# x split into its four phases by strided copies on 32 partitions, in place of a block transpose and a TensorE transpose

## The chip, the cores and the metric

The kernel runs on one core of a Trainium2 chip. The metric is the time of one execution on the device, in microseconds (us), as the median of several runs. TensorE, VectorE, ScalarE and GpSimd are called PE, DVE, ACT and POOL in the profile, and SP is the engine whose queue issues most of the loads.

## The reference

x has the shape (128, 32, 512): 128 samples, 32 channels, length 512. Two layers are added to it, each a conditioned mixing of channels and a feed-forward part.

```python
# layer 0
h = conv1d(x, weight, kernel 9, pad 4, 4 groups of 8 channels) + (cond @ c_weight.T)[:, :, None] + fside
logits = h @ W_gate + b_gate                 # over the length: D = 512, 8 experts
top 2 experts of each of the 4096 tokens (sample, channel)
x = x + mean over the 2 of relu(h @ W_e[e] + b_e[e])
# layer 1
att = softmax(mlp(cond))                     # 8 kernels
g = einsum(att-mixed 32x32 kernel, x) + att @ bias_k
x = x + g @ dequant(qweight, scales, zeros) + bias     # int4 weights, 512 x 512
```

## The kernel before, in words

The 128 samples are taken in NG = 32 groups of SUB = 4, so that a group is 128 tokens (sample, channel) of length 512. There are three stages.

**Stage 1, one step for each group.** The convolution is done on TensorE with time on the contraction's other side: the length is cut into PH = 4 phases (position l is 4 i + q), and `phases[q * 32 + channel, buffer, sample, 1 + i]` holds them, with a zero column at either end. Three shifts of that tile against the weights `wconv` give the convolution of one sample, so a group takes 4 x 3 matmuls into `ps_conv`. Around it, a group a goes through these steps:

- SP loads x of the group into `xt[:, a % 4, :]` (a ring of XR = 4), 128 rows of 2 KB (L376, L403).
- VectorE transposes it in blocks of 32 x 32 into `ring_a` (`transpose_x`, L694), reading every fourth element.
- TensorE transposes `ring_a` in four pieces into the PSUM bank `ps_ph` (`transpose_phases`, L1098).
- ScalarE copies `ps_ph` into `phases` (L567).
- TensorE convolves (L1169). VectorE adds the context: `hT` (L807).
- TensorE multiplies `hT` with the gate weights and an identity beside them (`gate_and_rows`, L1157). This gives the logits and the rows of h back in token order. The next group's gate waits for `tok_ready`, ScalarE's two copies of those rows into `token_list` (L584), and for VectorE's `partial` sums (L816).
- VectorE finds the top 2 experts, TensorE counts ranks (L1143, L1144), VectorE works out the two row numbers (L845), ScalarE copies the token's keys (L574), and GpSimd scatters the rows into the experts' lists in DRAM with two indirect DMAs (L524).

The order on each engine is written out by hand. In step g TensorE does: convolution g, transposes of g + 1, ranks of g - 2, gate of g - 1. VectorE does: hT g, block transpose g + 2, then the small operations of g - 1 and g - 2. ScalarE does: phases g + 1, keys g - 2, rows g - 1. `phases` and `ring_a` have two buffers each. In the last groups (from 24 on) a small network on the conditions runs between these steps, with two table loads and three activations on ScalarE (L600, L603, L606).

SP's queue loads x of group a + 4 once group a is transposed; between them it issues the experts' weights (1 MB a time, L385), the context (L400) and zeroed list heads (L390).

**Stage 2.** The lists are worked off in 71 blocks of 128 tokens: SP loads a block from the lists into a slot of `xt` (`list_step`, four loads L434 and one of keys L437), VectorE transposes it (L921), TensorE multiplies it with its expert's weights (L1196), VectorE adds the bias (L935), ScalarE applies the ReLU (L620), GpSimd scatters the results. On VectorE the first list transposes stand between the last steps of stage 1: list 0 comes ahead of step 30, list 1 ahead of step 31. The list loads of the first four blocks wait until the slots of `xt` have been read, through `xT_ready`.

**Stage 3** adds the two results of each token to x and does layer 1.

Program text that matters: before its first step TensorE, VectorE and ScalarE prepare the convolution's weights: ScalarE and VectorE pick the taps with six small copies each (`pick_taps`, L363), 32 partitions x 128 elements read 60 bytes apart.

## Time and profile before

| | us |
|---|---|
| median of 3 runs | 514.61 (514.56 to 514.78) |
| the profiled execution: its own time | 515.17 |
| the profiled execution: span of the trace | 513.4 |
| TensorE busy | 496.1 (97%) |
| VectorE busy | 347.0 (68%) |
| ScalarE busy | 121.0 (24%) |
| GpSimd busy | 153.3 (30%) |

Busy shares are means over three stages with different loads. Stage 1 reaches from the start to about 150 us, stage 2 to about 395 us. "PEld" is the loading of TensorE's stationary operand, which overlaps its matmuls. The granted clock is 1.00 at TensorE's full speed.

### The profile page before, as it was taken

What the parts mean: (1) busy time and instruction counts of PE and PEld (TensorE: products, weight loads), DVE (VectorE), ACT (ScalarE), POOL (GpSimd) and SP (SyncE); (2) the same over time, 40 slices, a digit from 0 to 9 for tenths busy, and PEclk for the clock granted to TensorE, in tenths of its full rate; (3) what the DMA queues carried; (4) which work ended last, traced back from release to release, by engine and by line L of the source; (5) the groups of instructions that cost most, each with busy time, mean ns of one, the idle gap of its engine ahead of it and who ended that gap; (6) DMA issues with size and microseconds to landing.
All of it is one profiled execution on the core that took longest, in us unless ns stands there. A gap on an engine that the chain in (4) does not pass through costs nothing. (4 is left out here: it accounts for less than half of the span.)

```text
span 513.4 us, 10342 instructions
## 1 busy us (share of the span) xinstructions
PE 496.1 (97%) x2412; PEld 329.5 (64%) x2413; DVE 347.0 (68%) x1082; ACT 121.0 (24%) x277; POOL 153.3 (30%) x178
## 2 busy tenths in 40 slices
PE   6999999999999999999999999999997999999996
PEld 5999999999964444444444444444544676767674
DVE  4588888888866547573354445444445899999996
ACT  3232333334421111111111111111123222222220
POOL 9144444444447322233323323332224000000000
PEclk9999999999998999999999999999999999999999
DMA  4969978999885686676665767675554798888852
GB/s 111 290 216 291 274 270 287 324 364 324 235 220 165 200 229 156 166 203 172 176 176 162 184 163 200 163 188 158 150 147 141 252 343 278 288 284 281 296 180 102
DMA packets 91442, 113.07 MB, mean 220 GB/s; under 512 B 25438, under 2 KB 62222, under 8 KB 90372
## 3 DMA queue, kind: packets, MB, share of 16 engines
q1 hardware_dynamic: 73200, 71.26, 49.3%
q0 software_dynamic: 11664, 36.24, 19.3%
q10 hardware_dynamic: 6536, 5.10, 3.5%
q8 instruction: 16, 0.26, 0.2%
q14 instruction: 26, 0.21, 0.1%
HBM read 67.55 MB, written 46.52 MB: 222 GB/s over the span
## 5 line engine op out<-in xcount | busy, mean ns | idle before, releaser
L1196 PE MATMUL bank<-we,lT 128*128 x536 | 233.6, 597 | 1.7 <-DVE ring_a L935 1.6
L1196 PEld LDWEIGHTS bank<-we,lT 128*128 128x128 f32 x536 | 101.7, 191 | 129.0 <-issue 128.8
L935 DVE TENSOR_TENSOR ring_a<-bank,be_bc 128x512 f32<-128x512 f32 x71 | 48.9, 690 | 104.4 <-PE bank L1196 50.4
L541 POOL DMA_INDIRECT pairs_d<-ring_b,pair_i x71 | 71.1, 1002 | 161.3 <-DVE pair_i L924 113.7
L1169 PE MATMUL bank<-wconv,phases 128*128 128x128 f32 x768 | 91.8, 276 | 0.7 <-ACT phases L567 0.7
L620 ACT ACTIVATE ring_b<-ring_a 128x512 f32<-128x512 f32 x71 | 44.7, 631 | 196.7 <-DVE ring_a L935 181.5
L1169 PEld LDWEIGHTS bank<-wconv,phases 128*128 128x128 f32 x768 | 89.1, 193 | 0.9 <-ACT phases L567 0.9
L524 POOL DMA_INDIRECT lists_d<-token_list,row_i x64 | 62.9, 983 | 83.6 <-DVE row_i L845 50.1
L921 DVE STREAM_TRANSPOSE lT<-xt 128x512 f32<-128x512 f32 x71 | 49.8, 702 | 5.7 <-DMA keys<-lists_d 5.4
L1263 PE MATMUL bank<-wq,high 128*128 128x512 f32 x128 | 37.4, 414 | 3.4 <-PEq L1211 3.4
L1157 PE MATMUL bank<-wg,lT 128*128 128x136 f32 x256 | 37.4, 289 | 1.1 <-DVE partial L816 1.1
L694 DVE STREAM_TRANSPOSE ring_a<-xt 128x512 f32<-128x512 f32 x32 | 35.3, 1102 | 0.0
L1267 PE MATMUL bank<-wq,low 128*128 128x512 f32 x128 | 34.5, 391 | 0.0
L567 ACT COPY phases<-bank 128x512 f32<-128x512 f32 x32 | 19.2, 600 | 64.5 <-PE bank L1098 49.2
L807 DVE TENSOR_TENSOR lT<-bank,rows_r 128x512 f32<-128x512 f32 x32 | 22.1, 690 | 16.3 <-PE bank L1169 13.1
L1157 PEld LDWEIGHTS bank<-wg,lT 128*128 128x128 f32 x256 | 31.8, 190 | 1.3 <-issue 1.2
L1242 PE MATMUL bank<-mix_bd,we 128*128 128x128 f32 x224 | 32.2, 287 | 0.0
L1242 PEld LDWEIGHTS bank<-mix_bd,we 128*128 128x128 f32 x224 | 27.3, 191 | 5.7 <-DVE we L1048 5.6
L584 ACT COPY token_list<-bank 128x256 f32<-128x256 f32 x64 | 20.7, 376 | 31.0 <-issue 17.1
L1267 PEld LDWEIGHTS bank<-wq,low 128*128 128x128 f32 x128 | 24.0, 188 | 5.5
L675 ACT CAST high<-bank 128x512 fp32r<-128x512 f32 x32 | 18.7, 586 | 36.3 <-PE bank L1242 36.3
L1263 PEld LDWEIGHTS bank<-wq,high 128*128 128x128 f32 x128 | 21.8, 190 | 7.0 <-issue 4.2
(194 smaller groups left out, 401.4 us busy)
## 6 DMA issues: line engine op xcount, KB each, us to landing
xt<-lists_d SPq DMA_DIRECT2D x284, 64.0 KB
xt<-in_x SPq DMA_DIRECT2D x60, 256.0 KB, 4.1
we<-pairs_d SPq DMA_DIRECT2D x28, 512.0 KB, 4.8
we<-in_L_ffn_W_e SPq DMA_DIRECT2D x8, 1024.0 KB
out<-orow_list SPq DMA_DIRECT2D x32, 256.0 KB, 2.8
lists_d<-orow_list SPq DMA_DIRECT2D x8, 257.0 KB
be_bc<-in_L_ffn_b_e ACTq DMA_DIRECT2D x4, 512.0 KB
words<-pairs_d POOLq DMA_DIRECT2D x4, 512.0 KB, 5.4
```

The lines of the kernel that those rows point to most:

```text
L524: pool.indirect_dma_start(lists_d, bass.IndirectOffsetOnAxis(ap=row_i[:, j, k:k + 1], axis=0), token_list[:, j, :], None, bounds_check=E * ...
L541: pool.indirect_dma_start(pairs_d, bass.IndirectOffsetOnAxis(ap=pair_i[:, s % DR:s % DR + 1], axis=0), ring_b[:, s % U, :], None, bounds_c ...
L620: act.activation(ring_b[:, j, :], ring_a[:, j % 2, :], ACT.Relu, scale=0.5).then_inc(result_ready, 1)
L694: dve.transpose(ring_a[:, ja % 2, :].rearrange("m (h q i) -> m q h i", h=MH, q=PH), xt[:, ja, :].rearrange("c (h l q) -> c q h l", h=MH, q ...
L921: dve.transpose(lT[:, ja, :].rearrange("m (p h r) -> m h p r", p=PH, h=MH), xt[:, ja, :].rearrange("r (h p l) -> r h p l", h=MH, p=PH)).th ...
L935: dve.tensor_tensor(ring_a[:, j % 2, :], ps_exp[j % 2][:, :], be_bc[:, bass.ds(expert, 1), :].rearrange("p a n -> p (a n)"), ALU.add).then ...
L1157: mm = pe.matmul(ps_both[:, p // 2, cols], hT[:, ja % 2, p * P:(p + 1) * P], wg[:, p, :], start=True, stop=True)
L1169: mm = pe.matmul(ps_conv[j % 2][:, s * P:(s + 1) * P], phases[:, j % 2, s, t:t + P], wconv[:, t, :, :].rearrange("k p o -> k (p o)"), star ...
L1196: mm = pe.matmul(ps_exp[j % 2][:, :], lT[:, j, p * P:(p + 1) * P], we[:, bass.ds(expert, 1), p, :].rearrange("m a n -> m (a n)"), start=(p ...
L1242: mm = pe.matmul(ps_mix[a % 2][:, q * P:(q + 1) * P], y_of(a)[:, q * P:(q + 1) * P], mix_bd[:, a, :], start=True, stop=True)
L1263: pe.matmul(ps_lin[j][:, :], high[:, j % 2, q * P:(q + 1) * P], wq[:, q, :], start=(q == 0), stop=False, skip_group_check=True)
L1267: mm = pe.matmul(ps_lin[j][:, :], low[:, j % 2, q * P:(q + 1) * P], wq[:, q, :], start=False, stop=(q == PH - 1), skip_group_check=True)
```

## The change

x is loaded with the channels on 32 partitions: slot i of the ring is now `x_quad[i]`, partitions 32 i to 32 i + 31 of `xt`, each holding the four samples' rows (4 x 512) of its channel. No transpose is needed then, since `phases` has channels on its partitions too. Each of the four phases is one copy of 32 partitions x 4 samples x 128 elements, which reads every fourth element and writes them side by side. VectorE copies phase 0 (`split_x`), ScalarE phases 1 to 3, one group further ahead than its copy before (group g + 2 in step g). The transposes on TensorE and the bank `ps_ph` go. The convolution now waits for the splits of both engines, the splits wait for the convolution two groups back, x loads wait for both splits of their slot, and the loads of the first four lists wait for both splits of the last group.

```diff
+        x_sub = x.rearrange("(g s) c l -> g c s l", s=SUB)
+        x_quad = [xt[i * C:(i + 1) * C, :, :] for i in range(XR)]
...
+        def split_phase(copy, q, jq, jb):
+
+            return copy(phases[q * C:(q + 1) * C, jb, :, 1:P + 1],
+                        x_quad[jq].rearrange("c s (l q) -> c q s l", q=PH)[:, q, :, :])
...
-                sp.dma_start(xt[:, g, :], x_g[g]).then_inc(x_in[g], 16)
+                sp.dma_start(x_quad[g], x_sub[g]).then_inc(x_in[g], 16)
...
-                    sp.wait_ge(xT_ready, k * XR + j + 1)
-                    sp.dma_start(xt[:, j, :], x_g[bass.ds(k * XR + XR + j, 1)].rearrange("a p l -> p (a l)")).then_inc(x_in[j], 16)
+                    sp.wait_ge(act_split, k * XR + j + 1)
+                    sp.wait_ge(dve_split, k * XR + j + 1)
+                    sp.dma_start(x_quad[j], x_sub[bass.ds(k * XR + XR + j, 1)].rearrange("a c s l -> c (a s) l")).then_inc(x_in[j], 16)
...
                     if isinstance(a, int) and a < XR:
-                        sp.wait_ge(xT_ready, NG - XR + a + 1)
+                        sp.wait_ge(act_split, NG)
+                        sp.wait_ge(dve_split, NG)
...
             def step1(g, j):
-                a = g + 1
+                a = g + 2
                 if live(a, NG):
 
-                    wait(act, ph_done, a + 1)
+                    ja = (j + 2) % U
+                    wait(act, x_in[ja], ring_count(a, ja, XR))
                     wait(act, conv_done, a - 1)
-                    act.copy(phases[:, (j + 1) % 2, :, 1:P + 1].rearrange("k s (h l) -> k h s l", h=MH),
-                             ps_ph[:, :].rearrange("k (h s l) -> k h s l", h=MH, s=SUB)).then_inc(ph_ready, 1)
+                    for q in range(1, PH):
+                        ins = split_phase(act.copy, q, ja, j % 2)
+                    ins.then_inc(act_split, 1)
...
-            stepped(act, step1, -1, lo1, hi1, NG + 2)
+            stepped(act, step1, -2, lo1, hi1, NG + 2)
...
-            def transpose_x(a, ja):
+            def split_x(a, ja):
 
                 wait(dve, x_in[ja], ring_count(a, ja, XR))
-                wait(dve, ph_done, a - 1)
-                dve.transpose(ring_a[:, ja % 2, :].rearrange("m (h q i) -> m q h i", h=MH, q=PH),
-                              xt[:, ja, :].rearrange("c (h l q) -> c q h l", h=MH, q=PH)).then_inc(xT_ready, 1)
+                wait(dve, conv_done, a - 1)
+                split_phase(dve.tensor_copy, 0, ja, ja % 2).then_inc(dve_split, 1)
...
-            def transpose_phases(a, ja):
-
-                wait(pe, xT_ready, a + 1)
-                wait(pe, ph_ready, a)
-                for h in range(MH):
-                    mm = pe.transpose(ps_ph[:, h * P:(h + 1) * P], ring_a[:, ja % 2, h * P:(h + 1) * P], ident[:, :])
-                mm.then_inc(ph_done, 1)
...
             def step1(g, j):
                 if live(g, NG):
 
-                    wait(pe, ph_ready, g + 1)
+                    wait(pe, act_split, g + 1)
+                    wait(pe, dve_split, g + 1)
                     wait(pe, hT_ready, g - 1)
...
-                if live(g + 1, NG):
-                    transpose_phases(g + 1, j + 1)
-
```

## Rows read from the trace of the kernel before

**Rows 1.** The page's slices: busy tenths of TensorE and its granted clock

```profile
PE   6999999999999999999999999999997999999996
...
PEclk9999999999998999999999999999999999999999
```

**Rows 2.** Windows of stage 1 and of stage 2

```profile
core 0: us, PE busy (x) PEld busy (x) DVE busy (x) ACT busy (x) POOL busy (x), PEclk, DMA share, GB/s
20.36:113.13 92.77, 92.54 (x839) 91.65 (x838) 77.52 (x378) 29.28 (x88) 40.68 (x42) 1.00 0.88 288
...
100.00:120.00 20.00, 20.00 (x184) 19.96 (x183) 17.40 (x94) 7.82 (x22) 8.89 (x10) 1.00 1.01 372
...
240.00:380.00 140.00, 140.00 (x341) 62.93 (x340) 62.48 (x134) 25.70 (x41) 42.09 (x44) 1.00 0.63 169
```

**Rows 3.** Timeline of TensorE: convolutions of groups 2 and 24 (start, us, ...)

```profile
20.36 2.87 PE L1169 MATMUL bank<-wconv,phases 128*128 128x128 f32 x24
...
113.13 2.84 PE L1169 MATMUL bank<-wconv,phases 128*128 128x128 f32 x24
```

**Rows 4.** Timeline of TensorE, one step

```profile
83.88 2.84 PE L1169 MATMUL bank<-wconv,phases 128*128 128x128 f32 x24
86.56 0.60 PE L1098 MATMUL bank<-ident,ring_a 128*128 128x128 f32 x4
87.00 0.17 PE L1143 MATMUL bank<-chosen,before 128*128 128x8 bf16 x1
...
88.06 0.61 PE L1169 MATMUL bank<-wconv,phases 128*128 128x128 f32 x4
```

**Rows 5.** VectorE: groups of the page, and single lines (ns min/median/max)

```profile
L694 DVE STREAM_TRANSPOSE ring_a<-xt 128x512 f32<-128x512 f32 x32 | 35.3, 1102 | 0.0
...
L363 DVE COPY words<-words x6: 244/298/872, 6.0 to 7.4; 32x128 f32<-32x128 f32 x6
...
L735 DVE CAST wq<-orow_list x4: 427/530/639, 199.8 to 205.1; 128x512 fp32r<-128x512 int32 x4
```

**Rows 6.** Timeline of ScalarE, one step

```profile
83.02 0.60 ACT L567 COPY phases<-bank 128x512 f32<-128x512 f32 x1 [2.04 <-issue]
...
83.51 0.19 ACT L574 COPY token_list<-expert_of 128x2 f32<-128x2 f32 x1
...
84.45 0.65 ACT L584 COPY token_list<-bank 128x256 f32<-128x256 f32 x2 [0.75 <-issue]
```

**Rows 7.** ScalarE: groups by line (busy, mean ns), and the taps' timeline

```profile
L363 ACT COPY words<-words 32x128 f32<-32x128 f32 x6 | 2.0, 409 | 3.2 <-DMA words<-in_L_cond_weight 3.2
...
L557 ACT COPY g<-ident 128x1 f32<-128x1 f32 x1 | 0.2, 191 | 0.0
...
L620 ACT ACTIVATE ring_b<-ring_a 128x512 f32<-128x512 f32 x71 | 44.7, 631 | 196.7 <-DVE ring_a L935 181.5
...
5.98 1.99 ACT L363 COPY words<-words 32x128 f32<-32x128 f32 x6 [3.24 <-DMA words<-in_L_cond_weight]
```

**Rows 8.** Timeline of TensorE: convolutions of groups 0 and 1

```profile
11.59 3.50 PE L1169 MATMUL bank<-wconv,phases 128*128 128x128 f32 x24
...
16.21 2.94 PE L1169 MATMUL bank<-wconv,phases 128*128 128x128 f32 x24 [0.69 <-ACT phases L567]
```

**Rows 9.** ScalarE, groups from 100 to 140 us: the small network

```profile
L600 ACT ACT_TABLE_LOAD x1 | 1.3, 1283 | 0.0
L606 ACT ACT_TABLE_LOAD x1 | 1.3, 1283 | 0.0
L603 ACT ACTIVATE g<-bank,b_sb 128x128 f32<-128x128 f32 x1 | 0.4, 384 | 0.0
```

**Rows 10.** Timeline at the end of stage 1; DMA issues (KB, us to landing)

```profile
129.36 2.08 SPq L434 DMA_DIRECT2D xt<-lists_d  x4
...
141.59 0.70 DVE L921 STREAM_TRANSPOSE lT<-xt 128x512 f32<-128x512 f32 x1
...
148.39 1.17 PE L1157 MATMUL bank<-wg,lT 128*128 128x136 f32 x8 [1.05 <-DVE partial L816]
...
bg_bc<-in_L_ffn_b_gate ACTq DMA_DIRECT2D x1, 4.0 KB, 2.6
```

More of the change, by code:

```diff
@@ L239, in build_program @@
         bank += [ctx.enter_context(nc.psum_tensor(f"bank{i}", [P, 512], F32)) for i in (6, 7)]
-        ps_ph, ps_conv, ps_rank, ps_misc = bank[1], bank[2:4], bank[6], bank[7]
+        ps_conv, ps_rank, ps_misc = bank[2:4], bank[6], bank[7]
         ps_exp = bank[2:4]
@@ L276, in build_program @@
         deq = sem("deq")
-        xT_ready = sem("xT_ready")
-        ph_done = sem("ph_done")
-        ph_ready = sem("ph_ready")
+        act_split = sem("act_split")
+        dve_split = sem("dve_split")
         conv_done = sem("conv_done")
@@ L398, in _ @@
                     if j == 2:
-                        sp.wait_ge(xT_ready, k * XR + 3)
+                        sp.wait_ge(act_split, k * XR + 3)
                         sp.dma_start(ctx_bc[:, cols], ctx_row[:, cols].to_broadcast((P, CTX_PIECE))).then_inc(ctx_in[2], 16)
-                    sp.wait_ge(xT_ready, k * XR + j + 1)
-                    sp.dma_start(xt[:, j, :], x_g[bass.ds(k * XR + XR + j, 1)].rearrange("a p l -> p (a l)")).then_inc(x_in[j], 16)
+                    sp.wait_ge(act_split, k * XR + j + 1)
+                    sp.wait_ge(dve_split, k * XR + j + 1)
+                    sp.dma_start(x_quad[j], x_sub[bass.ds(k * XR + XR + j, 1)].rearrange("a c s l -> c (a s) l")).then_inc(x_in[j], 16)
                 load_we(k + 1)
@@ L706, in _ @@
             pick_taps(dve.tensor_copy, range(PH // 2), dve_taps)
-            transpose_x(0, 0)
+            split_x(0, 0)
             for t in range(SHIFTS):
@@ L770, in rank_split @@
                 deq_step(dve.scalar_tensor_tensor(terms_w[:, :], full_low, odd[0:RK, 0:1], full, ALU.mult, ALU.add))
-            transpose_x(1, 1)
+            split_x(1, 1)
             dve.wait_ge(consts, N_CONSTS)
@@ L811, in step1 @@
                 if live(g + 2, NG):
-                    transpose_x(g + 2, (j + 2) % U)
+                    split_x(g + 2, (j + 2) % U)
                 if live(a, NG):
@@ L1115, in _ @@
                 mm.then_inc(wT_done, 1)
-            transpose_phases(0, 0)
             warm_up(WARM_START)
```

## The prediction

> **What bounds the kernel now.** I read the page's slices first, then stretches of the first stage, then single steps.
>
> In the slices TensorE stands at nine tenths almost everywhere and its granted clock is full [rows 1], so only what shortens TensorE's own sequence, or makes it wait, moves the time. The change lies in the first stage, so I take its steady part from the windows: from the start of convolution 2 (20.36 us) to that of convolution 24 (113.13), TensorE is busy for 92.54 of 92.77 us while VectorE is busy for 77.52 and ScalarE for 29.28 [rows 2]. The 22 steps between those two starts [rows 3] give 92.77 / 22 = 4.217 us a step. One undisturbed step in order of time is 4.18 us [rows 4]: the convolution takes 83.88 to 86.56 = 2.68, the four transposes of the next group's phases 86.56 to 87.00 = 0.44, ranks and gate 87.00 to 88.06 = 1.06. The remaining 0.04 of the mean is small stalls.
>
> VectorE at 77.52 / 22 = 3.52 us a step has 0.7 to spare, ScalarE at 1.33 has 2.9 to spare. The DMA engines' busy share is 0.88. These are the three that can inherit the bound.
>
> **What is removed.** On TensorE the four transposes: 0.44 us a step, on the path. TensorE's step alone becomes 3.74. On VectorE the block transpose, 1.10 us [rows 5]. On ScalarE one PSUM copy; it holds the engine 0.49 us, from 83.02 to 83.51 [rows 6].
>
> **What is added on ScalarE: three copies a step, 32 x 512, that read every fourth fp32 (16 bytes apart).** No row shows this shape. The nearest on the same engine are the tap copies at L363: 32 partitions, read 60 bytes apart, 409 ns for 128 elements, while VectorE copied from the same partitions [rows 7]. A one-element copy takes 191 ns [rows 7], so an element costs (409 - 191) / 128 = 1.70 ns, against (631 - 191) / 512 = 0.86 in the contiguous 512-element operation [rows 7]. A copy of 512 is then 191 + 512 x 1.70 = 1.06 us. Six L363 copies span 1.99 us, so they start (1.99 - 0.409) / 5 = 0.316 apart, 0.09 less than one lasts; mine start 0.97 apart. ScalarE's new step: 3 x 0.97, the key copy 0.19 - 0.09, the pair of row copies 0.65 - 0.10 [rows 6]: 2.91 + 0.10 + 0.55 = 3.56 us. Bounds: if the stride costs nothing, a copy is 0.63 and the step 2.26; at the rate of VectorE's block transpose, which reads xt 16 bytes apart too, taken as (1102 - 191) / 512 = 1.78 ns [rows 5], the step is 3.69; if a copy were four whole L363 copies (1.63 us), it is 5.27. I take 3.56, since L363 is the same engine and operation on the same number of partitions, and a fixed part need not be paid four times.
>
> The Trainium skill ("SBUF — State Buffer", Door 1, on cachelines) says that each access that crosses to a new 16-byte line pays, and adds that a stride of 4 fp32 is free. The first half would have my copies pay as L363 does, and the trace agrees for 60 bytes; the second half would give the free-stride rival below.
>
> **What is added on VectorE: one such copy.** Its L363 copies are 244 ns at least, 298 in the middle and 872 at most [rows 5]. The fastest leave little room for a stride penalty; four of the middle ones are 1.19 us, a slope through them and the 427 ns of a contiguous 512-element cast [rows 5] gives about 0.6. I take 0.7; the step becomes 3.52 - 1.10 + 0.7 = 3.1, hidden under 3.74. The 872 came beside GpSimd memsets, and the cast at L735 goes from 427 to 639 ns over its four instances. If each split lost 0.6 that way the step is 3.7, still hidden; this costs nothing in the sum.
>
> **The waits.** The order on ScalarE is splits of g+2, keys of g-2, rows of g-1. The splits wait for convolution g, and TensorE's gate of group g waits for the rows of g-1, which stand behind the splits in ScalarE's queue. So there is a chain over two steps: convolution g done, ScalarE's step (3.56), gate g and convolution g+2 (3.74 together with the ranks), plus hand-overs. I estimate these at 0.25 (the 0.10 by which the last copy outlasts its slot, and three signals of 0.05). Half of it is (3.56 + 3.74 + 0.25) / 2 = 3.78 us; with the small stalls of today, 3.82. The scatter on GpSimd waits for rows and row numbers and moves with them. SP's next x load waits for both splits, about 2.4 us later than for the transpose; the ring is four groups deep, 15 us, so nothing waits for it.
>
> **Start.** ScalarE ends its taps at 5.98 + 1.99 = 7.97, the first splits at 10.9; convolution 0 starts at 11.0 (before: 11.59). The splits of group 1 end at 13.9, so convolution 1 follows convolution 0 directly, at about 14.4 instead of 16.21 [rows 8]. Splits 2 wait for convolution 0 and end at 17.5; convolution 2 starts near 18.4 instead of 20.36. That is -2.0 us. The load of the gate bias, behind the first two splits on ScalarE's queue, comes later and costs up to 1 of this.
>
> **End of the stage.** Convolution 24 then starts at 18.4 + 22 x 3.82 = 102.4, against 113.13: -10.7. From there the small network on ScalarE adds two table loads of 1.28 and three activations of about 0.35 [rows 9], 3.6 us, which had been hidden in idle time. Splits 26 start at 102.4 + 2.7 = 105.1; five steps of 3.56 and the 3.6 later, splits 31 start at 126.5 and end at 129.5. Here a wait is added: every list load, also the first, now waits for the splits of group 31, since slot 0 of the lists spans all partitions. Today the first list load is issued at 129.36, behind the transpose of group 28, and is in time for VectorE at 141.59 [rows 10]. Now it goes out at about 129.9; five issues of 0.52, the last landing 2.6 us after its start as the gate bias did [rows 10]: 134.6. VectorE's first list transpose stands in its queue ahead of the hT of group 30, so gates 30 and 31, and with them stage 2, wait. From 134.6: list transpose 0.7, the rest of a VectorE step 3.52 - 1.10 = 2.4, the second list transpose 0.7, then hT, partial sums and rows of the last groups, which I put at 1.6 (the 0.65 of the row copies [rows 6] and the first third of a VectorE step): gate 31 at 140.0, against 148.39 [rows 10]. Stage 2 starts that much sooner and has no part in the change.
>
> **Sum.** Start -2.0, 22 steps of 4.217 - 3.82 = 0.40: -8.7, network and late lists +2.3 (from -10.7 to -8.4). In all -8.4. The profiled execution took 515.17 us (span 513.4), 0.56 over the median of 514.61: 506.8 for it, 506.2 for the median.
>
> **Rivals.**
>
> *The stride is free* (step of ScalarE 2.26). TensorE alone sets 3.78, the network is hidden again, splits 31 end some 4 us earlier: 502.5. For it: VectorE's 244 ns. Against: ScalarE's 409 ns for 128 elements. By the second half of the Trainium skill's sentence on lines ("SBUF — State Buffer", Door 1) this is what happens. 0.08.
>
> *ScalarE sets the pace, still faster.* Per element 1.8 to 2.0 ns, step 3.7 to 4.0: 508.5 to 513. For it: 0.18 us of distance to TensorE's step is thin, and ScalarE, VectorE and TensorE would read these partitions together. 0.12.
>
> *ScalarE becomes the bound and the kernel slower.* Each 0.1 us of its step costs 22 x 0.1 in the steady part, 0.5 after it. From 3.56 to 3.82 only half counts in the steady part. The balance tips at a step of about 4.08, that is 2.04 ns an element. At 2.1 ns (step 4.18) it is some 518; at the upper bound, 5.27, it is 547. Against: L363 already had VectorE on the same partitions. 0.12.
>
> *The DMA engines become the bound.* x is 0.262 MB of the 288 x 4.217 = 1.21 MB that a step moves, 22%. The engines' 0.88 x 4.217 = 3.71 us a step hold 0.80 of x. If packets to 32 partitions take twice as long, it is 4.51: x or scatters come late and the steady pace is 4.5, some 523 in all. It decides from about 1.6 times on. Against: 372 GB/s from 100 to 120 us at a share of 1.01, with TensorE busy for all 20 us, and stage 2, whose list pieces go to 32 partitions each, at 0.63 for 169 GB/s [rows 2]. 0.11.
>
> By the Trainium skill ("SBUF — State Buffer", Door 1) 32 partitions reach 8 of 16 ports, 189 GB/s against 328 for 1 MiB. By that figure x's packets would cost up to 1.7 times as much, a step 4.3 us and the kernel some 517, an estimate from that page; no row here shows such a transfer.
>
> **How the numbers follow.** Forecast 0.57, the rivals 0.08, 0.12, 0.12, 0.11. A difference under 0.2% (1 us) can't be told from none. Where the second and the third rival meet, 0.01 of each lies within it. Faster: 0.57 + 0.08 + 0.11 = 0.76; same 0.02; slower: 0.11 + 0.11 = 0.22. The forecast's own range is 503 to 510.5 (bounds 0 and 1.78 ns of the stride). The range of 8 in 10 reaches from just under the free stride, 502.0, to 516.5, which leaves out the DMA case and the upper part of the third rival.
>
> **What the profile after would show.** Right: no idle of TensorE ahead of the convolutions beyond 0.1 us, convolutions 3.8 apart, ScalarE's splits of 1.06 us, ScalarE over 90% busy in the stage, a first list transpose that waits for its DMA, and TensorE idle for 2 to 3 us ahead of gate 30. Wrong: splits of over 1.2 us and gates waiting for the row copies (ScalarE), splits waiting for x or rows waiting for a scatter (DMA), VectorE's split over 1.3 us.

## The result, and the profile after

The changed kernel takes 523.74 us (median of 4 runs, 522.89 to 526.25) against 514.69 for the kernel before on the same chip (4 runs, 514.56 to 515.64): a ratio of 1.0167, 95% interval 1.0135 to 1.0199. It is slower by 9 us where 8.4 us less was forecast. The profiled executions took 522.89 (span 521.1) and 515.17 (span 513.4).

The page's slices of the changed kernel, busy tenths of ScalarE and TensorE and TensorE's granted clock, against [rows 1]:

```profile
PE   6999999998859999999999999999997999999996
...
ACT  6899999999911211111111111111222222222220
...
PEclk9999999999978999999999999999999999999999
```

ScalarE now stands at nine tenths through stage 1, and a hole in TensorE's row with a fallen clock lies at its end (the twelfth slice, 143 to 156 us; the clock is down in the next one too). The same stretches as windows, cut at the starts of convolutions 2, 24 and 31 and of the second expert product (columns as in [rows 2]):

```profile
0.00:20.74 20.74, 15.59 (x88) 14.48 (x90) 11.63 (x19) 13.67 (x18) 13.74 (x38) 1.00 0.68 159
20.74:113.11 92.37, 86.23 (x751) 83.51 (x750) 71.73 (x378) 90.77 (x132) 41.65 (x41) 1.00 0.93 284
113.11:145.74 32.63, 28.56 (x247) 27.45 (x246) 22.55 (x133) 31.04 (x49) 14.04 (x15) 1.00 0.74 255
145.74:163.00 17.26, 11.18 (x52) 8.41 (x51) 7.21 (x39) 2.33 (x8) 5.06 (x6) 0.70 0.63 169
```

From convolution 2 to 24 ScalarE is busy for 90.77 of 92.37 us (before: 29.28 of 92.77 [rows 2]), and the 22 steps take 92.37 / 22 = 4.20 us each (before: 4.22). The last window is half empty on TensorE, at a granted clock of 0.70. Put beside the prediction's terms:

| term | forecast | measured |
|---|---|---|
| start of convolution 2 | -2.0 | +0.4 (20.36 to 20.74) |
| 22 steps | -8.7 | -0.4 (92.77 to 92.37) |
| conv 24 to conv 31 (the small network) | in the next | +2.4 (30.24 to 32.63) |
| conv 31 to the second product (late lists) | +2.3 with the network | +7.7 (9.87 to 17.58) |
| the rest of the span | 0 | -2.4 (360.16 to 357.78) |
| sum | -8.4 | +7.7 (513.4 to 521.1) |

The medians differ by 1.3 us more than the spans, because the profiled execution of before was 0.5 above its median and that of after 0.85 below.

**One step of TensorE** in order of time, against [rows 4]:

```profile
79.82 2.84 PE L1170 MATMUL bank<-wconv,phases 128*128 128x128 f32 x24
82.50 0.18 PE L1143 MATMUL bank<-chosen,before 128*128 128x8 bf16 x1
...
82.97 1.17 PE L1157 MATMUL bank<-wg,lT 128*128 128x136 f32 x8 [0.26 <-ACT token_list L595]
83.97 2.84 PE L1170 MATMUL bank<-wconv,phases 128*128 128x128 f32 x24
```

The four transposes and their 0.44 us are gone, and convolution follows convolution after 4.15 us where it was 4.18. In their place the gate waits for `token_list`, ScalarE's row copies: 0.26 us in this step, 0.28 and 0.29 in its neighbours. **The step of ScalarE** says why, against [rows 6]:

```profile
82.85 3.38 ACT L370 COPY phases<-xt 32x512 f32<-32x512 f32 x3
86.26 0.19 ACT L585 COPY token_list<-expert_of 128x2 f32<-128x2 f32 x1
86.36 0.64 ACT L595 COPY token_list<-bank 128x256 f32<-128x256 f32 x2
87.02 2.24 ACT L370 COPY phases<-xt 32x512 f32<-32x512 f32 x2
```

No line has a bracket: ScalarE doesn't idle between them. From one set of splits to the next it is 87.02 - 82.85 = 4.17 us: 3.41 for three splits, 0.10 to the row copies, 0.66 for these. One split lasts, on either engine (ns min/median/max):

```profile
L370 ACT COPY phases<-xt x96: 1093/1114/1139, 8.1 to 142.7; 32x512 f32<-32x512 f32 x96
L370 DVE COPY phases<-xt x32: 592/615/5799, 8.0 to 140.8; 32x512 f32<-32x512 f32 x32
```

**The end of stage 1**, against [rows 10]: TensorE, SP and VectorE, and then TensorE's windows with the granted clock (third number from the end):

```profile
144.02 1.86 SPq L443 DMA_DIRECT2D xt<-lists_d  x4
146.06 1.48 SPq L446 DMA_DIRECT2D keys<-lists_d  x1
```

```profile
150.27 0.71 DVE L930 STREAM_TRANSPOSE lT<-xt 128x512 f32<-128x512 f32 x1 [6.43 <-DMA keys<-lists_d]
```

```profile
145.74 2.84 PE L1170 MATMUL bank<-wconv,phases 128*128 128x128 f32 x24
153.61 0.19 PE L1143 MATMUL bank<-chosen,before 128*128 128x8 bf16 x1 [5.02 <-DVE chosen L863]
...
153.71 2.15 PE L1157 MATMUL bank<-wg,lT 128*128 128x136 f32 x8
156.92 2.15 PE L1157 MATMUL bank<-wg,lT 128*128 128x136 f32 x8 [1.05 <-ACT token_list L595]
158.86 4.57 PE L1194 MATMUL bank<-we,lT 128*128 x8
```

```profile
148.00:150.00 2.00, 0.58 (x6) 0.39 (x4) 0.00 (x0) 0.00 (x0) 0.00 (x0) 1.00 0.46 132
150.00:152.00 2.00, 0.00 (x0) 0.00 (x0) 1.71 (x6) 0.19 (x1) 0.00 (x0) 0.64 0.47 99
...
154.00:160.00 6.00, 4.95 (x18) 4.14 (x18) 3.61 (x21) 1.49 (x5) 3.34 (x4) 0.50 0.68 173
```

The first list goes out at 144.02, right behind the last splits, and is there 6.25 us later, when VectorE transposes it. VectorE idles 6.43 us for it, then does everything queued behind, and TensorE idles 5.02. During that idle its granted clock falls to 0.50, the lower level (1.2 of 2.4 GHz), and it stays there until 160: the gates take 2.15 us (before 1.17 [rows 10]) and the first product 4.57 (before 3.70).

### The profile page after: what moved, and what is told of

It is laid out like the page before. It is cut to its first block and busy times, and to the rows that moved or that the text cites. A ratio compares the mean times of both kernels' runs of the same rounds, so it can differ in the third digit from the quotient of the medians.

```text
span 521.1 us, 10146 instructions
## 1 busy us (share of the span) xinstructions
PE 490.1 (94%) x2284; PEld 320.7 (62%) x2285; DVE 343.3 (66%) x1082; ACT 209.1 (40%) x341; POOL 156.0 (30%) x178
## 5 line engine op out<-in xcount | busy, mean ns | idle before, releaser
L370 ACT COPY phases<-xt 32x512 f32<-32x512 f32 x96 | 107.1, 1115 | 3.8 <-PE bank L1170 2.3
L1170 PE MATMUL bank<-wconv,phases 128*128 128x128 f32 x768 | 93.8, 280 | 0.5 <-ACT phases L370 0.5
L533 POOL DMA_INDIRECT lists_d<-token_list,row_i x64 | 64.7, 1011 | 91.5 <-ACT token_list L595 65.0
L1170 PEld LDWEIGHTS bank<-wconv,phases 128*128 128x128 f32 x768 | 91.1, 197 | 0.9 <-ACT phases L370 0.9
L1157 PE MATMUL bank<-wg,lT 128*128 128x136 f32 x256 | 39.2, 298 | 9.1 <-ACT token_list L595 8.9
L1157 PEld LDWEIGHTS bank<-wg,lT 128*128 128x128 f32 x256 | 33.5, 198 | 11.2 <-issue 8.6
L679 ACT CAST rows_r<-bank 34x128 fp32r<-34x128 f32 x32 | 8.3, 258 | 46.1 <-PE bank L1247 46.1
L370 DVE COPY phases<-xt 32x512 f32<-32x512 f32 x32 | 25.0, 780 | 1.1 <-DMA xt<-in_x 0.4
```

The costliest lines, as they stand in the source:

```text
L370: return copy(phases[q * C:(q + 1) * C, jb, :, 1:P + 1], x_quad[jq].rearrange("c s (l q) -> c q s l", q=PH)[:, q, :, :])
L533: pool.indirect_dma_start(lists_d, bass.IndirectOffsetOnAxis(ap=row_i[:, j, k:k + 1], axis=0), token_list[:, j, :], None, bounds_check=E * ...
L1157: mm = pe.matmul(ps_both[:, p // 2, cols], hT[:, ja % 2, p * P:(p + 1) * P], wg[:, p, :], start=True, stop=True)
L1170: mm = pe.matmul(ps_conv[j % 2][:, s * P:(s + 1) * P], phases[:, j % 2, s, t:t + P], wconv[:, t, :, :].rearrange("k p o -> k (p o)"), star ...
```

## The experiments

They ran in four groups, each beside the kernel before on the same chip (medians of before 515.1 us for e1, e2, e3 and e5, 515.7 for e4, e6, e7 and e8, 515.9 for e9, e10 and e11, 515.6 for e12). Ratios are to that, and by this scale the changed kernel stands at 1.0167. Where two ratios from different groups are set against each other, look at the starts of stages beside them. Three kernels (e3, e4, e10) compute other values: the text says which.

### The steady step: stride, division of the work, DMA

**e3, consecutive reads.** The splits read 128 consecutive elements in place of every fourth, so that `phases` holds the wrong phases (and tokens go to other experts).

```diff
-                        x_quad[jq].rearrange("c s (l q) -> c q s l", q=PH)[:, q, :, :])
+                        x_quad[jq].rearrange("c s (q l) -> c q s l", q=PH)[:, q, :, :])
```

> The changed kernel with its eight split copies reading 128 contiguous elements at a time in place of every fourth: same sizes, same partitions, but the phases hold other positions of x, so the convolution's values and with them the routing differ; its stages, not its total, are to be read. Theory (the 16-byte stride is what makes ScalarE's copy 1.11 us): the copy falls to 0.63 to 0.70 us, ScalarE's step to 2.7, the pace to about 3.8. Rival (the copy is slow because of the few partitions, the writing rows or the sharing with other engines): the copy stays at 1.0 us or more and the pace at 4.1.

Measured: 512.73 us, 0.9939 (0.9914 to 0.9964). The same copies and one step of ScalarE:

```profile
L370 ACT COPY phases<-xt x96: 613/616/619, 8.0 to 130.9; 32x512 f32<-32x512 f32 x96
L370 DVE COPY phases<-xt x32: 403/415/5505, 8.0 to 130.3; 32x512 f32<-32x512 f32 x32
```

```profile
81.21 1.87 ACT L370 COPY phases<-xt 32x512 f32<-32x512 f32 x3 [1.24 <-PE bank L1170]
83.10 0.19 ACT L585 COPY token_list<-expert_of 128x2 f32<-128x2 f32 x1
83.19 0.64 ACT L595 COPY token_list<-bank 128x256 f32<-128x256 f32 x2
84.95 1.25 ACT L370 COPY phases<-xt 32x512 f32<-32x512 f32 x2 [1.11 <-PE bank L1170]
```

The stride alone costs ScalarE 1114 - 616 = 498 ns a copy, 0.97 ns an element, and VectorE 200 ns. Without it ScalarE waits more than 1 us for the convolution in the step shown, that step is 84.95 - 81.21 = 3.74, as long as TensorE's own, convolution 31 starts at 134.34 in place of 145.74, and the kernel is 2.3% (12 us) faster than with it. That the stride is what keeps the steady part from its gain is shown.

The mean step is longer, though. From convolution 2 (18.79) to 24 (106.55) it is 87.76 / 22 = 3.99 us: 3.74 holds in single steps only. The DMA engines are full in this stretch (the two numbers at the end are their share and GB/s):

```profile
20.00:60.00 40.00, 38.96 (x343) 37.67 (x342) 29.50 (x164) 26.06 (x61) 18.14 (x18) 1.00 1.00 290
60.00:100.00 40.00, 39.30 (x352) 38.52 (x351) 31.43 (x187) 26.00 (x61) 20.11 (x20) 1.00 0.99 320
```

ScalarE waits 4.6 us for scatters to land before it may write `token_list` again, and 2.8 us once for x. So the forecast's 3.82 isn't reached here, though the split is cheap.

The Trainium skill ("SBUF — State Buffer", Door 1, on cachelines) says both that each access to a new 16-byte line pays, and that a stride of 4 fp32 is free. Every element of this copy is on a line of its own: the measurements bear out the first half and contradict the second.

**e4, the loads alone.** The kernel before, with the 28 loads of x in the loop sent to 32 partitions of another buffer. The block transpose reads what the first four loads left, so the output differs.

```diff
-                    sp.dma_start(xt[:, j, :], x_g[bass.ds(k * XR + XR + j, 1)].rearrange("a p l -> p (a l)")).then_inc(x_in[j], 16)
+                    sp.dma_start(x_quad[j], x_sub[bass.ds(k * XR + XR + j, 1)].rearrange("a c s l -> c (a s) l")).then_inc(x_in[j], 16)
```

> The kernel before with its 28 later x loads going to 32 partitions each (in memory that nothing reads), while the transposes go on reading x of the first four groups; the values of stage 1 after group 3 and the routing differ, so its steps in stage 1, not its total, are to be read. Theory (the loads are hidden): steps of 4.18 to 4.22 us as before, no waits for x or for a scatter beyond those of before. Rival (32 partitions make x's packets up to twice as long): the DMA share rises from 0.88 towards 1.0 and steps become longer than 4.3 us, with waits for x_in or for scatters.

Measured: 515.51 us, 1.0001 (0.998 to 1.0022). The DMA engines' share from 60 to 100 us:

```profile
60.00:100.00 40.00, 39.96 (x365) 39.62 (x363) 33.71 (x165) 12.52 (x38) 18.65 (x19) 1.00 0.92 288
```

It was 0.89 at 289 GB/s in the kernel before; from 20 to 60 us it is 0.95 against 0.83, from 100 to 140 us 0.98 against 0.94. So the same bytes occupy the engines for 3 to 14% more time, and TensorE is busy throughout all the same. At steps of 4.2 us the DMA engines are not the bound: the rival is refuted for the changed kernel. At shorter steps it isn't: see e3 above, and e10.

**e2, two phases on each engine.**

```diff
-                    for q in range(1, PH):
+                    for q in range(2, PH):
...
-                split_phase(dve.tensor_copy, 0, ja, ja % 2).then_inc(dve_split, 1)
+                for q in range(2):
+                    ins = split_phase(dve.tensor_copy, q, ja, ja % 2)
+                ins.then_inc(dve_split, 1)
```

> The changed kernel with two phases copied by VectorE and two by ScalarE, in place of one and three. Theory (ScalarE's queue of 4.17 us a step sets the pace): ScalarE's step is 3.0 us, VectorE's 3.7, so TensorE's own 3.74 and the hand-overs set 3.8 to 3.9; 22 steps and the network part save 8 to 10 us, the list wait stays: 513 to 516 us. Rival (the DMA engines or x landing late set the pace): still 4.1 to 4.2 a step and 522 to 525 us. Rival (VectorE becomes the bound, its copies blocked by GpSimd): a step of 4.0 or more.

Measured: 523.04 us, 1.0144 (1.0125 to 1.0162), a miss. Waits from 21 to 140 us, first of TensorE, then of ScalarE (us in total, times, longest):

```profile
PE bank L1145 <- DVE chosen L865: 9.4, 15, 1.1
```

```profile
ACT phases L370 <- PE bank L1172: 21.9, 23, 1.3
```

ScalarE is relieved (22 us of waits), but now TensorE's rank counting waits for `chosen`, the last result of VectorE's step. In the steps that run in the loop with addresses from registers, VectorE goes from one `hT` to the next in 4.62 us (54.32 to 58.94) without a gap of over 0.3 us, although its busy share from 60 to 80 us is only 16.98 of 20: the small operations do not start as densely as their durations add up. In the steps written out one by one, from 87 us on, the pace is 4.04. I had put VectorE's step at 3.1 plus one copy. The kernel before shows the same: in its loop VectorE goes from `hT` to `hT` in 4.08 us (53.28 to 57.36) without waiting for another engine, so it had 0.1 us to spare there and not the 0.7 that its busy time suggests.

### The end of the stage: the list wait and the clock

**e1, x in a buffer of its own.** x is loaded into `ring_b`, whose only other use in stage 1 (the mixing weights) moves to two other tiles, so `xt` is free for the lists and their wait goes.

```diff
-        x_quad = [xt[i * C:(i + 1) * C, :, :] for i in range(XR)]
+        x_quad = [ring_b[i * C:(i + 1) * C, :, :] for i in range(XR)]
...
-        mixw_sb = ring_b[0:E, 0:2, :].rearrange("k h n -> k (h n)")
+        mixw_sb = [scale_bc[0:E, :], zero_bc[0:E, :]]
...
-                        sp.wait_ge(act_split, NG)
-                        sp.wait_ge(dve_split, NG)
```

> The changed kernel with x in memory of its own (that of ring_b, free in stage 1), so that the first four list loads wait for no split. Theory (the list wait at the end of the stage costs the time): the steady pace stays at 4.17 us, convolution 31 starts at about 145.7 as before, but the first list is loaded early, and the stretch from convolution 31 to the second expert product falls from 17.6 to about 10 us; the later part gives back the 2.4 us that it had gained; in all 517 to 519 us. Rival (list loads are slow by themselves after the change, or the clock falls anyway): TensorE still idles about 5 us ahead of gate 30 and the time stays at 522 to 525.

Measured: 516.45 us, 1.0026 (1.0009 to 1.0043). The last convolution and the first products:

```profile
146.56 2.84 PE L1168 MATMUL bank<-wconv,phases 128*128 128x128 f32 x24
153.04 3.70 PE L1192 MATMUL bank<-we,lT 128*128 x8 [0.36 <-issue]
156.63 3.68 PE L1192 MATMUL bank<-we,lT 128*128 x8
```

From convolution 31 to the second product it is 156.63 - 146.56 = 10.07 us, against 17.58 with the wait and 9.87 before. ScalarE's step stays at 4.17. The medians differ by 1.0167 - 1.0026 = 1.4%, 7.3 us: the list wait and what follows from it.

**e6, TensorE kept at work through the wait.** 40 transposes of the identity behind convolution 31; the list wait stays.

```diff
+                if isinstance(g, int) and g == NG - 1:
+                    warm_up(40)
```

> The changed kernel with 40 transposes of the identity into an unused bank put on TensorE behind convolution 31, where it idled for 5 us. Theory (the wait itself costs about 5 us and the fall of the granted clock to 0.5 behind it about 3 more): with TensorE busy in the gap the clock stays at 1.0 from 150 to 161, the last gates and the first product run at full speed, and the kernel gains 2.5 to 4 us: 519.5 to 521.5. Rival (the clock falls for another reason): the granted clock still shows 0.5 behind 150 us and the time is 523 to 526.

Measured: 519.18 us, 1.007 (1.0043 to 1.0097). A window of the wait, the gate behind it and the first product:

```profile
150.00:152.00 2.00, 1.74 (x18) 1.50 (x16) 1.89 (x13) 0.63 (x3) 0.17 (x1) 1.00 0.47 98
```

```profile
151.68 1.17 PE L1157 MATMUL bank<-wg,lT 128*128 128x136 f32 x8
...
155.03 3.70 PE L1196 MATMUL bank<-we,lT 128*128 x8
```

The clock stays at 1.00 and gate and product keep their old durations. The medians differ by 1.0167 - 1.007 = 0.97%, 5.0 us, but that is not the price of the clock, as convolution 31 and the second product show:

```profile
144.12 2.84 PE L1170 MATMUL bank<-wconv,phases 128*128 128x128 f32 x24
158.62 3.68 PE L1196 MATMUL bank<-we,lT 128*128 x8
```

This stretch is 14.50 us, against 17.58 with the fallen clock and 10.07 without the wait (e1). So of the 7.5 us that the list wait costs there, the wait itself takes 4.4 and the half clock 3.1. The rows agree: two gates of 2.15 in place of 1.17 and a product of 4.57 in place of 3.70 make 2.83. Another 1.6 us of e6's gain lie ahead of the edit: its convolution 31 starts at 144.12 in place of 145.74, because its start was faster (see e7).

The Trainium skill ("TensorE: Matmul & The Clock Gate", Part 1) says that an idle array is gated to half of its clock pulses until it has been busy for a time. The granted clock of 1.00, 0.64 and 0.50 in the windows above agrees.

**e5, the list wait in the kernel before.** Its first four list loads wait until the block transpose of group 31 is done.

```diff
-                        sp.wait_ge(xT_ready, NG - XR + a + 1)
+                        sp.wait_ge(xT_ready, NG)
```

> The kernel before with one change alone: the first four list loads wait for the transpose of group 31, as they wait for its splits in the changed kernel. Theory: the first list goes out at 140 in place of 129.4 and lands some 6 us later at 146 against 141.6, so the hT of group 30 and TensorE are late by about 4 us, with a fall of the granted clock after it: 517 to 521 us. Rival (the list loads have slack enough, the loss came from elsewhere): within 1 us of 514.6.

Measured: 518.02 us, 1.0052 (1.003 to 1.0074). In its profiled execution (514.76, the lowest of its nine) TensorE waits 1.12 us ahead of the rank counts at 147.60, the granted clock stays at 1.00, and the second product starts at 155.19, 1.95 after that of before. The first list goes out at 140.05, 3.6 ahead of convolution 31, where it is 1.7 ahead in the changed kernel. By the medians the same wait costs 0.52%, a third of e1's 1.4%. The total is as expected, but the 4 us and the fall of the clock don't show in this execution, and the slower ones have no trace.

### The start

**e7, GpSimd's memset later.** VectorE's longest split had lasted 5.80 us. The profile shows it beside the end of GpSimd's issues and its memset (VectorE, then GpSimd):

```profile
9.49 5.80 DVE L370 COPY phases<-xt 32x512 f32<-32x512 f32 x1
```

```profile
11.42 3.53 POOL L524 MEMSET mix_bd<- 128x4096 f32 x1
```

Here the memset (of `mix_bd`, used in stage 3) goes behind the scatters of stage 1.

```diff
-            pool.memset(mix_bd[:, :, :], 0.0).then_inc(mixbd_zero, 1)
...
+            pool.memset(mix_bd[:, :, :], 0.0).then_inc(mixbd_zero, 1)
```

> The changed kernel with GpSimd's clearing of mix_bd (3.5 us) moved from 11.4 us to behind the scatters of stage 1. Theory (VectorE's second split was held for 5.8 us by GpSimd's work, and this is why the start gained nothing): that split takes 0.6 to 1.5 us; convolution 1 does not start sooner, if TensorE's slow start is what holds it, and the gain is 0 to 1.5 us. Rival (the 5.8 us have nothing to do with GpSimd): the split stays at 5 us or more.

Measured: 526.0 us, 1.02 (1.0167 to 1.0232). No split of VectorE lasts over 737 ns, and convolution 2 starts at 18.89, 1.85 earlier. But ScalarE then meets x of group 4 late. By convolution 4 (29.16) 0.7 us of the lead are left, by convolution 31 (145.22) 0.5:

```profile
23.89 3.35 ACT L370 COPY phases<-xt 32x512 f32<-32x512 f32 x3 [1.00 <-DMA xt<-in_x]
```

Neither the faster start nor the longer total can be put down to the split. In e6, whose program is that of the changed kernel up to convolution 31, VectorE's split lasted 5.66 us, and yet:

```profile
11.41 6.78 PE L1170 MATMUL bank<-wconv,phases 128*128 128x128 f32 x48 [0.40 <-ACT phases L370]
...
18.95 2.92 PE L1170 MATMUL bank<-wconv,phases 128*128 128x128 f32 x24
```

The first two convolutions last 6.78 us where they last 8.42 in the changed kernel. The start thus differs between executions of the same code by as much as this edit seemed to bring. And the second product starts at 162.69, still 0.6 ahead: the 4.1 us by which e7's total is longer from there on (524.6 - 162.69 = 361.9, against 357.8) lie in stages 2 and 3. There the moved memset now stands ahead of the first result scatter of stage 2 (it begins at 177.69, in the changed kernel at 174.87), and TensorE idles for some 2 us from 178 to 182. Whether that is the whole of it isn't shown.

**e9, e1 with twelve warm-up transposes** ahead of convolution 0 in place of eight.

```diff
-            warm_up(WARM_START)
+            warm_up(12)
```

> The changed kernel with x in its own memory and twelve instead of eight identity transposes ahead of convolution 0, so that TensorE does not idle between 11.0 and 11.5 us. Theory (TensorE's pass through the first convolution at half rate until 17 us, where the kernel before had the full rate from 13 us, follows from that idle): convolution 0 takes 3.3 to 3.6 us in place of 5.6, convolution 2 starts 1.5 to 2 us sooner, and the kernel takes about 514.5 to 515.5 us. Rival (the rate rises at a time of its own that varies from run to run): convolution 2 starts anywhere between 18.5 and 20.6 and the median is that without the extra transposes, 516.4.

Measured: 516.52 us, 1.0028 (1.0008 to 1.0048), as e1. The first convolutions:

```profile
11.79 3.32 PE L1168 MATMUL bank<-wconv,phases 128*128 128x128 f32 x24
15.64 2.92 PE L1168 MATMUL bank<-wconv,phases 128*128 128x128 f32 x24 [0.53 <-DVE phases L370]
```

In the changed kernel TensorE idles 0.52 us ahead of convolution 0 and the first two convolutions together last 8.42 us (11.55 to 19.97). With the gap filled the first lasts 3.32, and convolution 2 starts at 19.32. That is later than in e6 (18.95), where the gap of 0.40 us was left, so that the warm-up made the difference isn't shown. Then the splits of group 4 wait 1.25 us for x at 23.95, and convolution 4 starts at 29.22, 0.6 ahead of that of e1 (29.85). In the profiled execution convolution 31 is 1.4 ahead (145.15 and 146.56), but the median shows no gain over e1: a miss, and the time that the rival gave.

### Combinations

**e8: e1, e2 and e7 together.** (Its diff is those three.)

> The changed kernel with x in its own memory, two phases on either engine, and GpSimd's clearing moved: all three costs taken away. Theory (these are the causes): pace 3.8 to 3.9, convolution 31 at about 136, no list wait: 504 to 508 us, below both kernels. Rival (something else, such as the DMA engines, takes over as the bound): 511 us or more, with scatters or weights landing late.

Measured: 520.35 us, 1.0097 (1.0071 to 1.0123), a miss. TensorE waits 10.6 us for `chosen` between 21 and 140 us: VectorE is the bound as in e2, now without the list wait. Its profiled execution (518.77) is the lowest of six, and it carries e7's moved memset too, whose cost in stage 2 isn't separated.

**e10: e1 and e3 together** (phases wrong as in e3).

> The changed kernel with x in its own memory and with contiguous reads in its split copies; the phases hold other positions of x, so values and routing differ. Theory (the stride sets ScalarE's step and so the pace, the list wait the end): pace 3.8 us, no list wait: convolution 31 starts near 133, the first product by 142, some 505 to 508 us. Rival (without ScalarE as the bound the DMA engines hold the pace): pace of 4 us or more and over 511.

Measured: 508.62 us (two runs), 0.9871 (0.9828 to 0.9913). Convolution 31 starts at 136.03, the first product at 142.54. With neither stride nor list wait the change gives 6.7 us; beside e1, the stride is worth 1.0026 - 0.9871 = 1.55%, 8 us (10.5 us at the start of convolution 31). The pace of 3.8 was missed: from convolution 2 (18.62) to 24 (107.71) a step takes 4.05, ScalarE waits 6.0 us for scatters and once 3.3 for x, and the DMA engines' share is 1.00. The rival's pace of 4 us or more with the DMA engines as the bound came true, its time of over 511 didn't.

**e11: e9, and from group 18 on two phases on each engine.** There the steps are written out and VectorE has room.

```diff
+        def late(a):
+
+            return isinstance(a, int) and a >= hi1 + 2
...
-                    for q in range(1, PH):
+                    for q in range(2 if late(a) else 1, PH):
...
-                split_phase(dve.tensor_copy, 0, ja, ja % 2).then_inc(dve_split, 1)
+                for q in range(2 if late(a) else 1):
+                    ins = split_phase(dve.tensor_copy, q, ja, ja % 2)
+                ins.then_inc(dve_split, 1)
```

> The changed kernel with x in its own memory, twelve identity transposes at the start, and two phases on either engine only from group 18 on, where the steps are written out. Theory (VectorE with two copies needs 4.6 us a step inside the loops with register-addressed operands, but 4.04 where the steps are written out): steps 16 to 29 take 4.05 in place of 4.17 and the network part loses its 2.4 us: 511.5 to 513.5 us, below the kernel before. Rival (VectorE's second copy costs as much as ScalarE's third saved): 514.5 to 516.5.

Measured: 513.35 us, 0.9961 (0.994 to 0.9981). From 82.46 to 110.81 the seven steps take 4.05 each, and convolution 31 starts at 142.06, ahead of that of the kernel before (143.37) and 4.5 ahead of e1. Of these 4.5 us 1.6 were there at convolution 4 (28.29 and 29.85), the start again; the rest came with the division of the work. This beats both kernels, by 0.4% the kernel before.

**e12: e11, with the first expert weights behind x of groups 4 and 5** on SP's queue.

```diff
-            load_we(0)
-            zero_head(0)
             with sp.Fori(0, NG // XR - 1) as k:
...
-                load_we(k + 1)
-                zero_head(k + 1)
+                load_we(k)
+                zero_head(k)
+            load_we(E - 1)
+            zero_head(E - 1)
```

> The kernel before it (own scratch memory, twelve warm-up transposes, two phases per engine from group 18 on), with the first 1 MB of expert weights and the list head issued on SP's queue behind x of groups 4 and 5 in place of ahead of them. Theory: in the runs with warm-up transposes the gain of the start was lost because x of group 4 lay behind those weights on SP's queue (the splits waited 1.25 us for it near 23.95 and convolution 4 started at 29.2); with the weights later there is no such wait, convolution 4 starts near 27.9, and the median falls by about 1.3 us to 511.5 to 513 (ratio 0.992 to 0.995 of the kernel before). Rival: x's landing only took the blame, the splits are held by ScalarE's own step of 4.17; then convolution 4 starts at 29 again and the time is that of the kernel before it, 513.3 (0.996). A second rival: the weights of the first experts now land late ahead of the first product, or hold later loads, and the time is slower than 514.

Measured: 512.11 us, 0.993 (0.9915 to 0.9945), the lowest of those with the right phases. But the mechanism is not the expected one. The expectation took convolution 4's start of 29.2 from e9; in e11 the splits of group 4 (23.02) had waited for x for 0.1 us at most, and it started at 28.29. In e12:

```profile
22.89 3.36 ACT L374 COPY phases<-ring_b 32x512 f32<-32x512 f32 x3
...
27.04 3.38 ACT L374 COPY phases<-ring_b 32x512 f32<-32x512 f32 x3
```

Convolution 4 starts at 28.16, 0.13 us earlier, with ScalarE's splits 4.15 apart already: the rival's reading (ScalarE's own step holds the start) is the right one here. The spans of e11 and e12 are 511.2 and 511.1, the first products start at 148.50 and 148.25, and the two ran on different chips with intervals that meet. That e12 is faster than the kernel before is shown; that it is faster than e11 is not.

A phase on GpSimd wasn't tried.

## Why the prediction was wrong

**The step that failed** is the size of one term: "2.91 + 0.10 + 0.55 = 3.56 us" for ScalarE's step. It measured 3.41 + 0.10 + 0.66 = 4.17. That takes 8.3 of the forecast's 8.7 us in the steady part. Of the slowdown of 1.67% e1 leaves 0.26, so what makes the kernel clearly slower is a second term that was too small, the list wait. Three things add up to the 0.61 of ScalarE's step:

- A copy lasts 1.114 us, not 1.06 (together 0.16). The rate from the tap copies, 1.70 ns an element, was near; the fixed 191 ns and 1.80 ns give what was measured.
- The copies start 1.13 apart, not 0.97 (3.41 - 2.91 = 0.50, less the 0.16). The 0.09 by which short copies overlap had been subtracted three times. The splits do not overlap at all, with a stride or without: in e3 they last 0.616 and start (1.87 - 0.616) / 2 = 0.627 apart.
- The row copies hold the engine for 0.66, not 0.55, since the split behind them doesn't overlap them either.

**What followed from it.** "ScalarE sets the pace" was a rival with a tipping point at a step of 4.08, and 4.17 lies beyond it. So the third rival came true, as a mechanism. Its number came out by two errors against each other: for a step of 4.18 it gave 518, with the late lists at their forecast price; with this step the changed kernel measured 523.7, and e1, which doesn't have the list wait, 516.5. And the rival was tied to the wrong quantity, the nanoseconds an element: at 1.8 ns it counted as "still faster, step 3.7", and its sign in the profile, "splits of over 1.2 us", did not show, though the other, gates waiting for the row copies, did. (Its sentence "From 3.56 to 3.82 only half counts" doesn't fit the prediction's own chain, (step + 3.74 + 0.25) / 2, by which half counts up to 3.99; the times that it gives are those of the chain.) The chance of 0.12 was low: the rate had been varied between bounds, while the overlap, worth a third of a microsecond, had been taken as known. The sentence "0.18 us of distance to TensorE's step is thin" had the warning in it: all three terms of a sum so close to the bound needed bounds.

**The list wait** was seen, and its kind was right: `act_split` for group 31, list transpose ahead of hT of group 30, gates behind it. Its size was wrong, +2.3 with the network against +10.1 measured (2.4 + 7.7). The network's part was right: seven steps of 4.17 and the 3.6 us make 32.8, measured 32.63, and ScalarE is busy for 31.04 of it. The list's part was not, by two sizes. The list was there 6.25 us after its issue (144.02 to 150.27), forecast were 4.7 (129.9 to 134.6). The issuing was right (the fifth load goes out 2.04 us after the first, forecast 2.1); its landing took 4.2 us where the 2.6 of the gate bias had been put in. And TensorE's idle of 2 to 3 us was priced as idle alone. It became 5.02 with a half clock behind it, worth another 3.1 us by e6. The kernel before has a slice of 8 in the clock's row too [rows 1], at its own change of stages, but it is no sign of the same thing: TensorE was busy for all of the 8 us from 154 to 162 there, while the granted clock fell to 0.50. What made it fall isn't settled.

**The start** was forecast at -2.0, measured +0.4. ScalarE and VectorE had their first splits ready almost as forecast (convolution 0 at 11.55, not 11.0), but the first two convolutions took 8.42 us, where those of the kernel before took 3.50 and 2.94 [rows 8], and ScalarE's splits of group 2, which wait for the first of them, began at 17.14. The forecast had given the first convolution its 3.4 us of before, without a reason why it should keep them. What decides this length is not shown. It is 6.78 us for the two in e6, with the same start as the changed kernel, and 6.4 to 7.1 in e7, e8, e10, e11 and e12; only in the changed kernel and in e1, where the idle ahead of them was longest (0.52 and 0.55 us), is it over 8. Part of such a lead was lost by convolution 4 in e7 and e9, where the splits met x late, and nearly none in e6 and e11 (convolution 4 at 28.20 and 28.29).

**VectorE's split** was 0.615, forecast 0.7, and the step was not the bound, as forecast. But it gained less than the 0.4 us a step that the sum gave it: from the start of hT to that of `partial` it is 1.42 us (82.75 to 84.17) where it was 1.63 (82.64 to 84.27), 0.2 less. The block transpose overlapped its successor and the copy does not. And "VectorE at 77.52 / 22 = 3.52 us a step has 0.7 to spare" was a wrong reading: busy time is not the length of a step, and in the loop it had 0.1 (see e2). That is why e2 and e8 found no room there.

**Removed work** was right: 0.44 us on TensorE; single steps of e3 and e10 show its own step of 3.74 to the hundredth. The pace of 3.82 made from it was not: the mean steps there are 3.99 and 4.05, so that of the 0.40 us a step at most 0.23 could be had, even with a cheap split. **DMA** at 0.11 was refuted by e4 for steps of 4.2 us, but the waits for scatters and x in e3 and e10, at a share of 1.00, make it a likely next bound, beside VectorE's step in the loop; no run separates the two. **The free stride** at 0.08 was refuted by e3. **The rest** was forecast at 0 and measured -2.4: stage 2 of before had a fall of its own, to 0.50 from 160 to 162 us and 0.71 to 164, and a wait of 1.59 us at 193.72, which the profiled execution of after doesn't show in this form (its clock falls earlier). Why they fell away isn't settled.

**What stays open:** why ScalarE's splits don't overlap while its short copies do, and what decides whether TensorE is at its full rate from 13 us on or only from 17.

## What to carry to other kernels

When work moves from the bounding engine to another, add up the receiving engine's new step with a bound on each term, overlap included. Where the sum comes within a tenth of the old step, let the term that was not measured for this shape decide the chances. Moving a 0.44 us step of TensorE onto an engine that pays 1.1 us a piece for it only changes which engine is the bound. And look at what a reused buffer spans: a layout that puts one group on a quarter of all slots makes every slot wait for the last group, and five microseconds of idle TensorE there cost three more in clock. And before a gain at the start is put down to an edit, compare two executions that start with the same code.

## What the runs showed of the hardware

- ScalarE copies 32 x 512 fp32 in 616 ns when it reads consecutively and in 1114 ns when it reads one element in 16 bytes; VectorE in 415 and 615 ns. The first agrees with the Trainium skill ("ScalarE: Activation LUTs", What ACT_TABLE_LOAD costs), whose 186 ns and 0.833 ns an element give 613.
- One fp32 copy of VectorE within SBUF lasted 5.80 us (usual 0.615) and ended 0.34 after GpSimd's memset of 3.53 us. It began 1.93 us ahead of the memset, beside GpSimd's issues of DMAs. With the memset moved away (e7) the longest was 0.74, but in e1, e11 and e12, which have memset and issues in their places, it wasn't held either (at most 0.78): what exactly held it isn't settled.
- TensorE at about half its rate while the granted clock reads 1.00: from 13 to 15 us the changed kernel issues 11 matmuls, the kernel before 20, in windows that both say 1.00; e6, with the start of the changed kernel, issues 17.
- With TensorE idle for 5.02 us the granted clock fell from 1.00 to 0.64 and 0.50; in the kernel before it fell to 0.50 from 160 to 162 us while TensorE was busy throughout (8.00 of 8.00 us from 154 on).
- Loads of 256 KB into 32 partitions in place of 128 raised the DMA engines' share by 3 to 14% in mixed traffic, and left the time where it was (e4, 1.0001).
